# Eight-feature heads: keys moved to their score rows by DMA, one maximum for two heads, GpSimd's steps spread over the slots

## The reference

```python
h = norm(x)
q, k, v = h @ wq + bq, kv @ wk + bk, kv @ wv + bv      # kv: h, or the context
s = einsum("bihd,bjhd->bhij", q, k) / sqrt(8) + mask   # 16 heads, d = 8, i and j up to 256
p = softmax(s, axis=-1)
x = x + concat_heads(p @ v) @ wo + bo                  # L0_attn: then a gated feed forward
```

## Time and profile before

| | |
|---|---|
| median of 3 runs | 3032.33 us (3031.67 to 3038.67) |
| the profiled execution's own time | 3037.95 us |
| its span, first to last instruction | 3036.1 us |
| mean granted TensorE clock | 0.822 of full speed |
| PE, DVE, ACT, POOL busy | 69%, 55%, 33%, 7% of the span |
| the four `attend8` sublayers, from their first to their last instruction | 267.7, 222.2, 294.2 and 223.2 us |
| from the first memset to the first cast of maxima (L472) | 47.3, 39.2, 50.0 and 39.3 us |

### The profile page before, as it was taken

One profiled execution on the slowest core, in us unless ns is written; L12 is line 12 of the kernel. 1 busy time (PEld: TensorE's weight loads), 2 busy tenths in 40 slices (PEclk: granted clock), 3 DMA queues, 4 the chain that ended last, 5 costly groups with the idle time before them and its releaser, 6 DMA issues. The chain is left out here.

```text
span 3036.1 us, 39171 instructions
## 1 busy us (share of the span) xinstructions
PE 2081.0 (69%) x12768; PEld 1151.9 (38%) x12854; DVE 1662.4 (55%) x5877; ACT 1013.1 (33%) x1920; POOL 222.3 (7%) x251
## 2 busy tenths in 40 slices
PE   4998679728874469982332677777698887569932
PEld 1554323315543325541122444444454444323310
DVE  3765357644444446557667656665633333437754
ACT  1454246521111135532200344443332222126621
POOL 3320032000000041100000000000000000021100
PEclk9998889959986679995555898998898988569965
DMA  1000010000000000000000100000000000000000
GB/s 64 2 2 2 0 42 2 8 0 0 0 6 0 0 25 2 1 11 0 36 0 0 78 3 3 3 3 3 8 1 0 0 0 5 0 7 1 2 1 14
DMA packets 8183, 25.51 MB, mean 8 GB/s; under 512 B 640, under 2 KB 3712, under 8 KB 7040
## 3 DMA queue, kind: packets, MB, share of 16 engines
q1 hardware_dynamic: 8064, 23.93, 2.3%
HBM read 22.88 MB, written 1.05 MB: 8 GB/s over the span
## 5 line engine op out<-in xcount | busy, mean ns | idle before, releaser
L412 DVE TENSOR_REDUCE L_xattn_nmax<-ps 128x2 f32<-128x512 f32 x384 | 259.5, 688 | 197.2 <-PE ps L605 194.2
L524 ACT ACTIVATE L_xattn_probs<-ps 128x1024 f32<-128x1024 f32 x192 | 196.5, 1024 | 129.3 <-PE ps L642 128.9
L678 PE MATMUL ps<-L_xattn_parts,lay 128*128 128x512 bf16 x517 | 167.2, 416 | 23.2 <-POOL L_xattn_parts L295 8.6
L2072 ACT ACTIVATE wide_pr<-wide_sc,wide_nm 128x256 f32<-128x256 f32 x256 | 127.9, 500 | 132.7 <-DVE wide_nm L2024 111.6
L1129 DVE SCALAR_TENSOR_TENSOR moe_z_sb<-ps,weights,moe_a_sb 128x512 f32<-128x512 f32 x64 | 47.7, 750 | 173.8 <-ACT moe_a_sb L1147 173.7
L605 PE MATMUL ps<-L_xattn_ks,L_xattn_qs 64*128 64x256 bf16 x768 | 132.7, 274 | 6.7 <-issue 5.1
L2020 DVE CUSTOM_DVE_ANT_0 wide_sc<-ps,wide_mask 128x256 f32<-128x256 f32 x256 | 97.1, 416 | 67.2 <-PE ps L2112 67.2
L1181 PE MATMUL ps<-moe_z_sb,weights 128*128 128x512 f32 x256 | 123.6, 628 | 8.9 <-DVE moe_z_sb L1129 8.9
L657 PE MATMUL ps<-L_xattn_probs,L_xattn_v 128*32 128x256 f32 x1536 | 122.7, 391 | 2.7 <-ACT L_xattn_pv L535 2.7
L2123 PE MATMUL ps<-const,wide_pr 128*128 128x128 f32 x512 | 90.0, 302 | 36.9 <-DVE wide_pr L2030 36.9
L2112 PE MATMUL ps<-wide_k,wide_q 64*128 64x256 f32 x512 | 71.9, 405 | 45.3 <-DVE wide_nm L2024 37.8
(11 more groups left out here) (491 smaller groups left out, 4618.9 us busy)
## 6 DMA issues: line engine op xcount, KB each, us to landing
weights<-in_packed_L_ffn SPq DMA_DIRECT2D x2, 2608.0 KB, 12.3
weights<-in_packed_L_xattn SPq DMA_DIRECT2D x2, 1316.0 KB, 7.4
wide_mask<-in_mask SPq DMA_DIRECT2D x8, 256.0 KB, 2.7
weights<-in_packed_L_ffn SPq DMA_DIRECT2D x1, 1540.5 KB, 10.1
weights<-in_packed_L_ffn SPq DMA_DIRECT2D x1, 1540.0 KB, 6.7
const<-in_packed_const SPq DMA_DIRECT2D x1, 1165.5 KB, 8.3
weights<-in_packed_L_xattn SPq DMA_DIRECT2D x6, 192.5 KB, 2.5
weights<-in_packed_L_attn SPq DMA_DIRECT2D x2, 576.5 KB, 8.3
```

Source lines behind the costliest of these rows:

```text
L412: v.tensor_reduce(nm, ps[:, BANK_M + j, :].rearrange("p (t n) -> p t n", t=2), AX.X, ALU.max, negate=True).then_inc(S("m_used"), 1)
L524: a.activation(probs[:, s % RING, :, :, :].rearrange("p j t n -> p j (t n)"), ps[:, BANK_P:BANK_P + 2, :], ACT.Exp, scale=HD ** -0.5)\
L678: mm = pe.matmul(ps[:, SIDE[bank], :], C.lay[:, n, part, gp * P:(gp + 1) * P], parts[:, n, part, :], start=part == 0, stop=part == 2)
L2072: ins = a.activation(pr[:, h % 2, qt, :], sc[:, h % 2, qt, :], ACT.Exp, bias=nm[:, h % 2, qt:qt + 1], accum_out=sums[:, h % 2, qt:qt + 1])
```

## The change

- **Keys.** The weights of the keys are permuted on the host (`by_rows`), so that the 64 projected features of one head parity lie as 8 features x 8 head pairs. SyncE then moves each bf16 part of the keys to its rows of `kk` by a DMA of 64 rows of 1 KB, 12 DMAs per pair of sequences (6 pairings x 2 halves). The 8 key tiles' matmuls, their ScalarE copies and their half of `lay` go away. Rows 48 to 63 and 112 to 127 must be one: VectorE sets rows 32 to 63 and 96 to 127 of `kk` to 1.0 at the start of each `attend8`, ahead of its wait for the weights.
- **Queries** keep `lay`, one tile in each place from 8 to 15 (9 to 16 in the causal case), all in one side bank: the first matmul of a tile waits until ScalarE has copied the tile before (`q_ready`).
- **Maxima.** One `max_scores` call makes both heads' scores and one `maximum` reduces both banks. In TensorE's slot the order is now turn values, turn maxima, weigh, one piece of side work, maximum scores, probability scores, the rest of the side work.
- **Normalising** goes from GpSimd to ScalarE (`centre`, `rescale`), GpSimd's split is cut into steps of one instruction, one a place; the masks' four instructions stand in four places. In the causal case the projections of the pair after next are made one a place in places 12 to 15, through one bank.

```diff
+def by_rows(wt):
+    return np.ascontiguousarray(wt.reshape(wt.shape[0], HEADS // 2, 2, HD).transpose(0, 2, 3, 1)).reshape(wt.shape)
...
+                sp.wait_ge(S("cleared"), CLEARED)
+                for m in range(PAIRS):
+                    sp.wait_ge(S("k_parts"), m + 1)
+                    if m >= 2:
+                        sp.wait_ge(S("p_ready"), WINDOW * (m - 1))
+                    for part_slot, part in enumerate(K_PARTS):
+                        for j in range(2):
+                            r0 = 64 * j + HD * part_slot
+                            sp.dma_start(kk[r0:r0 + HD, m % 2, :, :], parts[half[j], 1, part, :])\
+                              .then_inc(S("k_laid"), 16)
...
-                                ins = g.tensor_scalar(one, C.x[:, m * PAIR + t * D:m * PAIR + (t + 1) * D],
-                                                  mv[:, m % 2, t, 0:1], rstd[:, m % 2, 0, t:t + 1],
-                                                  ALU.subtract, ALU.mult)
+                        ins = a.activation(xn[:, (m * PT if rope else 0) + t, :],
+                                           C.x[:, m * PAIR + t * D:m * PAIR + (t + 1) * D], ACT.Identity,
+                                           bias=rstd[:, m % 2, 2, t:t + 1], scale=rstd[:, m % 2, 0, t:t + 1])
...
-                        v.tensor_reduce(nm, ps[:, BANK_M + j, :].rearrange("p (t n) -> p t n", t=2), AX.X, ALU.max,
-                                        negate=True).then_inc(S("m_used"), 1)
+                        v.tensor_reduce(nm, ps[:, BANK_M:BANK_M + 2, :].rearrange("p j (t n) -> p j t n", t=2), AX.X,
+                                        ALU.max, negate=True).then_inc(S("m_used"), 1)
...
+                for j in range(2):
+                    v.memset(kk[64 * j + 32:64 * j + 64, :, :, :], 1.0).then_inc(S("cleared"), 1)
                 v.wait_ge(C.weights_loaded[k], 32)
...
-                    for t, units in LAY.items():
+                    for gp in range(GP):
+                        t = Q_LAY + gp
                         m = p.job(t % WINDOW, 1 - t // WINDOW)
                         if m is not None:
-                            for n, gp, bank in units:
-                                free(m, t, bank)
-                                yield from lay(m, n, gp, bank)
+                            if gp == 0:
+                                pe.wait_ge(S("q_parts"), m + 1)
+                                if rope and m:
+                                    pe.wait_ge(S("q_ready"), GP * m)
+                            else:
+                                pe.wait_ge(S("q_ready"), GP * m + gp)
+                            for part in range(3):
+                                mm = pe.matmul(ps[:, BANK_A, :], C.lay[:, 0, part, gp * P:(gp + 1) * P],
+                                               parts[:, 0, part, :], start=part == 0, stop=part == 2)
+                                if part < 2:
+                                    yield
+                            yield mm.then_inc(S("q_laid"), 1)
...
                     if 0 <= s - 1 < SLOTS:
                         turn_max(s - 1)
-                    if 0 <= s - 2 < SLOTS:
-                        prob_scores(s - 2)
-                    g, kt = divmod(s - 4, 2)
+                    g, kt = divmod(s - 5, 2)
                     if 0 <= g < SLOTS // 2:
                         weigh_values(g, kt)
                     next(side, None)
                     if 0 <= s + 1 < SLOTS:
-                        max_scores(s + 1, 0)
-                    next(side, None)
-                    next(side, None)
-                    if 0 <= s + 1 < SLOTS:
-                        max_scores(s + 1, 1)
+                        max_scores(s + 1)
+                    if 0 <= s - 2 < SLOTS:
+                        prob_scores(s - 2)
                     for _ in side:
                         pass
```

More of the change, by code:

```diff
@@ L267, in attend8 @@
         slot = lambda s: (s // WINDOW, s % WINDOW // GP, s % GP)
-        places = [Place(tau, WINDOW, PAIRS) for tau in range(-2 * WINDOW, SLOTS + 11)]
+        places = [Place(tau, WINDOW, PAIRS) for tau in range(-2 * WINDOW, SLOTS + 12)]
         with C.turn() as block:
@@ new lines, in _ @@
+                for p in places:
+                    for stage, t, ahead, n in stages:
+                        m = p.job(t, ahead)
+                        if m is not None:
+                            stage(m, n)
+                    if boundary is not None:
+                        for b in range(2):
+                            for kt in range(2):
+                                m = p.job(10 + 2 * b + kt, 1)
+                                if m is not None:
+                                    if b == kt == 0:
+                                        g.wait_ge(S("ranks_ready"), 2 * (m + 1))
+                                        if m >= 2:
+                                            g.wait_ge(S("p_ready"), WINDOW * (m - 1))
@@ L351, in _, with newton @@
                 L = Link(v, S("vector_step"))
-                def newton(out, var, n, last):
+                def newton(out, var, n, done=None):
                     a, vv = C.nwt[0][:, 0:n], C.nwt[1][:, 0:n]
@@ L393, in prepare @@
                     L.settle()
-                    first, second = rstd[:, m % 2, 0, :], rstd[:, m % 2, 1, :]
-                    yield from newton(first, one[:, :, 1], PT, not rope)
+                    first, second, shift = (rstd[:, m % 2, n, :] for n in range(3))
+                    yield from newton(first, one[:, :, 1], PT)
+                    yield v.scalar_tensor_tensor(shift, one[:, :, 0], -1.0, first, ALU.mult, ALU.mult)\
+                        .then_inc(S("rstd_ready"), 1)
                     if rope:
@@ L604, in max_scores @@
                         for c0, c1 in ([(0, SEQ)] if not causal else [(0, P), (P, SEQ)][:qt + 1]):
-                            mm = pe.matmul(ps[:, bank, c + c0:c + c1], qs[half[j], m % 2, gp, q0:q0 + P],
-                                           kk[half[j], m % 2, gp, b * SEQ + c0:b * SEQ + c1], start=not masked,
-                                           stop=True, skip_group_check=masked)
+                            for j in range(2):
+                                mm = pe.matmul(ps[:, BANK_M + j, c + c0:c + c1], qs[half[j], m % 2, gp, q0:q0 + P],
+                                               kk[half[j], m % 2, gp, b * SEQ + c0:b * SEQ + c1], start=not masked,
+                                               stop=True, skip_group_check=masked)
                     mm.then_inc(S("m_ready"), 1)
@@ L673, in turn_values, with project @@
                     mm.then_inc(S("pv_turned"), 1)
-                def lay(m, n, gp, bank):
-                    pe.wait_ge(S(("q_parts", "k_parts")[n]), m + 1)
-                    for part in range(3):
-                        mm = pe.matmul(ps[:, SIDE[bank], :], C.lay[:, n, part, gp * P:(gp + 1) * P],
-                                       parts[:, n, part, :], start=part == 0, stop=part == 2)
-                        if part < 2:
-                            yield
-                    yield mm.then_inc(S(("q_laid", "k_laid")[n]), 1)
+                def project(m, bank, wt, src, done):
+                    pe.matmul(ps[:, bank, :], w(wt), src, start=True, stop=True).then_inc(S(done), 1)
@@ L2172, in _ @@
                 L(v.memset(C.lay[:, :, :, :], 0.0))
-                for n, order in enumerate((Q_PARTS, K_PARTS)):
+                for n, order in enumerate((Q_PARTS,)):
                     for slot, part in enumerate(order):
```

434 lines of the change are left out of this document (221 added, 213 removed).

## The result

The changed kernel takes 3086.4 us (median of 4; 3081.4 to 3089.3), the kernel before 3035.5 in runs on the same chip: ratio 1.0162, 95% interval 1.0135 to 1.0189. It is **51 us slower**. Forecast was 2967, 65 us under the median of 3032 that the prediction started from, with a range up to 3020.

The account below looks back on a forecast made before the run. TensorE was taken to bound laying slots and every masked slot, VectorE plain slots without laying, neither the prologue. Plain -36, masked -25, causal -33, prologues +29 made -65: 2967 us against the median; range 2940 to 2995, wider 2915 to 3020.

Parts of the forecast that it names:

- Weighing moved behind the turned maxima costs one change back: Masked loop: after cheaper masks and scores, the moved weighing adds one change of kind on TensorE, leaving -0.36 us a slot.
- is 1.72, under 1.98: Plain slots without laying: maximum, hand-over, scores, hand-over take 1.72 us, under VectorE's 1.98, so this loop doesn't bind.
- the round trip: Laying slots: the cycle from a tile's matmul through scores, exponentials and ScalarE's copies to the next tile, 2.7 us.
- 3.3 and 2: Full plain pair: 3.3 us won in eight laying slots, 2 in the eight others; given as 5.5 a pair.
- 1.30 less 0.87: Masked slot on TensorE: both heads' masks and scores fall from 1.30 to 0.87 us, priced at -0.36 with weighing moved.
- The merged maximum: Loops: one maximum takes 1.23 us for 1.29, a gain of 0.1 a VectorE-bound slot, 1.5 in the last plain pair.
- The clear: Prologue: two VectorE memsets cost by elements, 6.98 us each, 14.0 for both, delaying statistics by 10.6 us in L0_xattn.
- the clear is cheap by bytes: Rival: the memset costs by bytes, 7 us less in three prologues and 3.5 in L1_xattn: 2943 us, chance 0.14.
- The round trip that eats the laying slots: Rival: the laying slots' cycle takes 3.3 us instead of 2.7, ScalarE held by copies: 3012 us, chance 0.17.
- the slower ones: Two rivals: TensorE's clock stays low (3052 us), or few DMA engines make first slots wait (3075); together 0.09.
- The clock: Slower rival: TensorE, less busy, stays at granted clock 0.50 for a whole pair and some in each sublayer: 3052 us.
- signs of being wrong: Full pairs above 45 us, L0_xattn's first scores later than 46 us after its start, or SyncE's DMAs releasing them.

Follow-up runs that it names:

- e1: The changed kernel with ScalarE's copy of the weighed values one slot earlier, ahead of its slot's exponentials: 2983.8 us, ratio to the kernel before 0.9818.
- e2: The changed kernel with probability scores ahead of weighing and maximum scores on TensorE, the copy of values left in place: 2987.1 us, ratio to before 0.9831.
- e11: As e10, but with two maxima and each head's scores by themselves, next to each other on TensorE: 2944.5 us, ratio to the kernel before 0.9678.
- e5: The kernel before with only the merged maximum over both heads' banks, at the place of the second head's: 3062.9 us, ratio 1.0083.
- e10: The changed kernel with early value copy, score order by sublayer, word clear on VectorE behind first statistics, early query tiles in two banks: 2903.0 us, ratio to before 0.9544.
- e9: The kernel before with keys by the 12 DMAs alone, no key tiles, and the clear by words in VectorE's idle time: 2997.7 us, ratio 0.9853.
- e3: The changed kernel with VectorE's two memsets written as four-byte words, same bytes and place: 3050.3 us, ratio to the kernel before 1.0036.
- e12: As e10, but with normalising back on GpSimd, in the places it has on ScalarE: 2910.6 us, ratio to the kernel before 0.9579.
- e7: The changed kernel with the clear by four-byte words on VectorE, behind the first pair's statistics: 3028.7 us, ratio to the kernel before 0.9968.
- e4: The changed kernel with the clear by four-byte words on GpSimd, behind its own clears: 3044.1 us, ratio to the kernel before 1.0017.

## Why the prediction was wrong

**The step that failed** is in the masked loop and in the plain one at once: "Weighing moved behind the turned maxima costs one change back", and the loop of maximum and scores that "is 1.72, under 1.98". Both count TensorE's and VectorE's own work; what a moved probability score does to ScalarE was followed only for the tile's copy ("the round trip"), not for L535's copy of values, which was entered with its 0.28 / 2 and no waiter. The waiter is weighing, and the maximum scores stand behind it. The short slots are 1.73 us as worked out; every second one is 2.74. e1 and e2 put the price at 96 and 101 us in the four sublayers (103 and 99 by the medians), 12 and 10 of it in the drains, which were not in the sum at all (+13.1). Forecast and profile are 113 us apart: 79 in the loops, 13 in the drains, 13 before the first slots, 9 outside.

**The other steps of the loops held once that wait is out.** e1 tests them best, since TensorE's order is the change's there. Its 64 slots are 23.9 us less than before in each plain sublayer (-18 said), 20.6 in the masked (-25), 31.6 in the causal (-33): 100 for 94. Full plain pairs are 38.7 to 40.2 where 42 was said, masked 56 (56) from the second on, causal 50.4 and 41.5 (47). The last pairs, from first to last cast, fell from 31.5 to 28.7 and from 46.0 to 41.2 (-1.5 and -5.5 said). As it was run the plain loops gained 4, the causal 9, and the masked lost 2: of 94 us, 16 came. Two sums of the working are off by little: 3.3 and 2 are 5.3 a pair, not 5.5, and 1.30 less 0.87 with one change of 0.11 back is 0.32 a masked slot, not 0.36; e1's last masked pair gives 0.32.

**The merged maximum** takes 1.222 us (1.23 said). But its gain was put on VectorE, 3 us in two last pairs, and is small there (e11: 1 to 2 a plain sublayer); alone and in the old order it costs 25 (e5). Its part in the masked slot, 1.30 less 0.87, is 0.43 in the working and in the rows of e11 and e10; over 64 slots that would be 28, and e11 shows 20. The key tiles were worth 5.5 a full plain pair by the working; e9 gives 4.6 to 4.8 in the second and third.

**The clear** was mis-sized: +10.6 us to the statistics, measured +14.1, and these 3.5 us, four times, are about all by which the prologues missed (+41.7 for +28.6). The row's 0.85 ns was set above the Trainium skill's one cycle an element ("VectorE: DVE Perf Modes", section "Zero memsets can be issued as uint32 (trn2)"), which gave 8.5 each and "3 us more a sublayer". Start to start a memset is 8.65 us; the Trainium skill was right and the duration in the row is not the whole of it. The timeline of before had shown it, in the gap ahead of the row that I used (2.62 and 0.59 are 3.21 us for 3072 elements, 1.04 ns each):

```profile
16.21 2.62 DVE L2172 MEMSET lay<- 128x3072 uint32 x1 [0.59 <-issue]
```

That section of the Trainium skill gives the writing by words for zero and names no other value. That only zero may be written so was my reading of it, and e3, which writes ones so, contradicts it. The rival that the clear is cheap by bytes is out.

**The rest of the prologue**: tiles at 2.15 apart, as the earlier trace rows had them, and the granted clock 0.50 up to the first slots of L0_xattn (427.0 to 442.6), as said. Normalising in L0_attn -3.7 said, 4.6 in e12. L1_xattn's +1.2 for -3.5 is for 3.5 of its 4.7 the clear again. L0_attn came to +18.1 for +11; without the clear (e7) +4.7, so some 4 more than priced lie in the rest of it. That these are its projections is likely but not shown: no run splits them. The DMAs released nothing in the changed kernel, as forecast, but 4.9 us and "a few more to land" were 7.9 and 6.

**The rivals.** The round trip that eats the laying slots named the right engine and the wrong waiter: laying slots were 2.8 us on average in L0_xattn's third pair, its 2.7 was good. Of the slower ones, no DMA was waited for in the changed kernel. The clock did fall in part: L0_xattn's first and second pair had a mean granted clock of 0.92 and 0.96 where the kernel before had 1.00, some 10 us of its 64 slots at the lower level; no run tells what that cost. But it can't be the cause: e1 has nearly as much of it (9 us) and no loss. Of the signs of being wrong, the late first scores came (48.3 us for 46) and the plain full pairs stood at the edge (43.0 to 45.2 for 45); SyncE's DMAs released nothing. The slower case had another mechanism than the two that I priced.

## What to carry to other kernels

When an instruction is moved to the end of an engine's slot, follow it through its consumer's queue: whatever stands behind that consumer is late too, and its waiter may be at the head of the first engine's next slot. A loop closes only if every such cycle does, not just the one of the two busiest engines. Merging two halves costs where other work stands between the inputs (e5); with the inputs back to back it gained little on the engine that takes them (e11, plain) and more on the engine that makes them (e11, masked and causal). Put one-off clears behind the first dependent chain, not ahead of it, and on the engine that has nothing to lose by them.

## What the hardware showed unasked

- A memset's duration in the trace is short by a fifth: 6.88 us for 8192 elements, 3.47 for 4096, with "issue" gaps of 1.76 and 0.91 that grow with it.
- GpSimd's memsets held two VectorE TENSOR_SCALAR on 128 x 4 for 2.16 and 3.52 us (e4), while VectorE's own memset ran beside GpSimd's (396.10 beside 394.93, in the prologue above).
- An SBUF to SBUF DMA of 64 KB costs SyncE 0.66 us to issue (12 in 7.88), and the last of twelve landed some 6 us after its issue.
